# An adaLN and MoE block in fp32: the condition mixing's products in three fp32r passes, one table buffer, new instruction orders

## The reference

```python
# stage 0: a condition vector of each sequence makes a 128x128 matrix of rank 30
t   = x @ U(cond_512) + ub(cond_512)            # U from W_dec, b_dec;  [tokens, 30]
x0  = t @ V                                      # what the experts and the gate see
g   = top2_softmax(x0 @ Wg.T + bg)               # 8 experts, 2 used, computed densely
x1  = x + sum_e g_e * (gelu(x0 @ W1[e].T + b1[e]) @ W2[e].T + b2[e])
# stage 1: six conditions mixed by softmax(aw), three by tables, three by small MLPs
h   = layernorm(x1)
t_, s_, h_ = h * tm_g[ic], h * ms_g[im], layernorm(h * pw_g[ip] + pw_b[ip]) * cp_g[ic]   # rows of tables
z   = x1 @ Wx + t_ @ Wt + s_ @ Ws + h_ @ Wh + one-hot terms + terms of the sequence
y   = layernorm(silu(z) @ int_W2 + int_b2) * int_g + int_be
u   = silu(y @ w1 * s1) * (y @ w2 * s2)          # ternary weights
out = x1 + (gelu(gelu(u @ h1 * sh1) @ h2 * sh2) @ w3) * s3
```

## Time and profile before

| | |
|---|---|
| median of 3 runs | 433.07 us (431.69 to 435.24) |
| the profiled execution, its time | 432.53 us |
| the same, first to last instruction (span) | 430.6 us |
| busy PE, VectorE, ScalarE, GpSimd | 412.8, 313.0, 291.9, 115.1 us |
| granted TensorE clock, mean | 0.988 of full speed |

### The profile page before, as it was taken

The page is one execution under the profiler, slowest core; times in us unless marked ns, Lnnn a source line. Parts: engine busy times, 40 slices in busy tenths (PEclk is TensorE's granted clock), DMA queues, the critical chain, the costliest instruction groups (busy, mean ns, idle before and its releaser), DMA issues.

```text
span 430.6 us, 5742 instructions
## 1 busy us (share of the span) xinstructions
PE 412.8 (96%) x1804; PEld 270.1 (63%) x1804; DVE 313.0 (73%) x656; ACT 291.9 (68%) x518; POOL 115.1 (27%) x122
## 2 busy tenths in 40 slices
PE   6988999999999999999999999999999999898995
PEld 3755555545566765776567655776577657677774
DVE  4897899988995587658866757677963798656643
ACT  3687867877756864677646784786578475757653
POOL 0048102443525610244153000457035031110000
PEclk9996899999999999999999999999999999999999
DMA  6986547553443341334530260336402210000000
GB/s 232 356 355 210 140 102 193 138 171 105 128 124 107 107 129 50 105 73 107 141 99 32 57 164 0 89 69 175 153 0 65 73 56 0 2 0 24 2 24 27
DMA packets 30216, 45.07 MB, mean 105 GB/s; under 512 B 3717, under 2 KB 22634, under 8 KB 29674
## 3 DMA queue, kind: packets, MB, share of 16 engines
q1 hardware_dynamic: 25792, 32.88, 26.6%
q0 software_dynamic: 3584, 10.49, 7.5%
q10 hardware_dynamic: 810, 1.33, 0.9%
HBM read 40.68 MB, written 4.03 MB: 104 GB/s over the span
## 4 chain that ended last, share of the span: by engine, by line
PE 77%; DVE 9%; DMA 6%; issue 3%; ACT 3%; SPq 1%; POOL 1%; DVEq 0%; ACTq 0%; POOLq 0%
PE bank L752 21%; PE bank L650 20%; PE bank L788 7%; PE bank L698 7%; PE bank L642 5%; PE bank L737 5%; DMA gwbs<-gate_w 3%; PE bank L666 2%; PE bank L705 2%; DMA t_split<-tsS 2%; PE bank L830 2%; PE bank L777 1%; DMA Wd<-W_dec_in 1%; SPq L417 1%; PE bank L711 1%
## 5 line engine op out<-in xcount | busy, mean ns | idle before, releaser
L650 PE MATMUL bank<-mG,W 128*128 128x512 f32 x256 | 121.4, 600 | 0.2 <-DVE mG L1186 0.2
L897 ACT ACTIVATE mG<-bank,keepP 128x512 f32<-128x512 f32 x128 | 85.2, 687 | 29.3 <-PE bank L642 19.1
L1460 POOL TENSOR_TENSOR rstd<-ve,mhalf 128x4 f32<-128x4 f32 x24 | 32.7, 1364 | 206.3 <-DVE ve L1201 206.2
L1186 DVE TENSOR_TENSOR mG<-mG,gwbs 128x1024 f32<-128x1024 f32 x64 | 77.3, 1218 | 3.0 <-DMA gwbs<-gate_w 2.5
L650 PEld LDWEIGHTS bank<-mG,W 128*128 128x128 f32 x256 | 48.0, 192 | 40.0 <-issue 35.6
L642 PE MATMUL bank<-ts,A 96*128 96x512 f32 x128 | 64.5, 546 | 1.4 <-DVE A L1308 0.7
L962 ACT ACTIVATE G<-bank,keepP 128x512 f32<-128x512 f32 x48 | 32.1, 691 | 27.9 <-PE bank L752 27.8
L1441 POOL DMA_INDIRECT gp<-pgb_in,ixall x32 | 35.7, 1114 | 26.6 <-issue 9.2
L752 PE MATMUL bank<-hB_h,h2w_h 128*128 128x512 f32 x96 | 39.8, 414 | 0.0
L752 PE MATMUL bank<-hA_h,h1w_h 128*128 128x512 f32 x96 | 38.7, 403 | 0.0
L1444 POOL DMA_INDIRECT gcm<-ctm,ixcm x32 | 35.4, 1108 | 9.7 <-issue 9.4
(11 more groups left out here) (241 smaller groups left out, 775.8 us busy)
## 6 DMA issues: line engine op xcount, KB each, us to landing
gwbs<-gate_w SPq DMA_DIRECT2D x32, 512.0 KB
keep<-xT_in SPq DMA_DIRECT2D x8, 256.0 KB, 6.1
outT<-keep SPq DMA_DIRECT2D x8, 256.0 KB, 2.0
t_split<-tsS SPq DMA_DIRECT2D x7, 192.0 KB
ts<-t_split SPq DMA_DIRECT2D x7, 192.0 KB
W1T<-W1T_in SPq DMA_DIRECT2D x1, 1024.0 KB, 10.5
W<-W2T_in SPq DMA_DIRECT2D x1, 1024.0 KB, 13.3
hs<-h1T_in SPq DMA_DIRECT2D x1, 1024.0 KB, 11.6
```

The lines of the kernel that those rows point to most:

```text
L650: mm = pe.matmul(OACC[:, :], W2[:, e * HC + c, :], mG[n % NMG][:, c, :], start=False, stop=(e == E - 1 and c == HC - 1))
L897: act.activation(mG[e % NMG][:, c % HC, :], HM[n % 2][:, :], ACT.Gelu, bias=b1c[:, c:c + 1]).then_inc(m_gelu, 1)
L1186: dve.tensor_tensor(mine, mine, gate.unsqueeze(1).broadcast_to([P, HC, TT, P]), ALU.mult).then_inc(m_q, 1)
L1460: step(pool.tensor_tensor(rstd[:, n, :], ve[:, n, :], mhalf[:, :], ALU.pow))
```

## The change

- In Z, t, s and h are split like the feed-forward's data: ScalarE's copy out of XE writes the fp32r part (`turned_hi`), a new VectorE step (`tl`, `sl`, `hl`) the rest (`turned_lo`), also from XE. Z has three fp32r products for each (weight high by data high, high by low, low by high) in place of one fp32 product; the product with x1 stays in fp32 (`wx`). XE is free for the next turn when `tl`, `sl` or `hl` is done. `zl` splits the weights once, behind a copy on ScalarE.
- One buffer for the gathered tables instead of two; the place goes to `turned_lo`. The gathers of block b wait until t, s and h of block b-1 have been made.
- W_dec is the first load on SyncE's queue; the two small loads that stood before it are first on ScalarE's.
- All orders are written anew. Weight splits `wl` go in another sequence. A step `filler` is defined, but stands in no order.

The diff, its orders cut to those that are spoken of:

```diff
         w3 = [sb(f"w3_{p}", [P, FC, P], F32R) for p in "hl"]
-        wmix = sb("wmix", [P, 4, P])
+        wx = sb("wx", [P, P])
+        wc = [sb(f"wc_{p}", [P, 3, P], F32R) for p in "hl"]
...
         wsc = sb("wsc", [P, 6, P], stack=early)
+        wcf = sb("wcf", [P, 3, P], stack=early)
...
         mG = [mGs[:, i * HC:(i + 1) * HC, :] for i in range(NMG)]
-        gcm, gp = [None, None], [None, None]
-        gcm[0] = sb("gcm0", [P, TT, 3 * P])
-        gp[0] = sb("gp0", [P, TT, 2 * P])
+        gcm = sb("gcm", [P, TT, 3 * P])
+        gp = sb("gp", [P, TT, 2 * P])
...
         xh, tt, ss, hh = [norms[:, i, :, :] for i in range(4)]
-        ct, cs_, ch = [sb(f"c{k}", [P, T]) for k in "tsh"]
+        turned_hi = [sb(f"c{k}_h", [P, T], F32R) for k in "tsh"]
...
         nmr = sb("nmr", [P, 3, TT])
-        gp[1] = sb("gp1", [P, TT, 2 * P])
-        gcm[1] = sb("gcm1", [P, TT, 3 * P])
+        turned_lo = [sb(f"c{k}_l", [P, T], F32R) for k in "tsh"]
+        sb("spare", [P, 992])
...
         tr_mm = sems("tt_mm", "ss_mm", "hh_mm")
-        tr_out = sems("t_out", "s_out", "h_out")
+        tr_out, tr_lo = sems("turned_hi", "turned_lo")
+        wc_hi, wc_lo = sems("wc_hi", "wc_lo")
...
                 "y_mm", "yT_mm", "f_full", "f_hi", "f_lo")
-        gat = sems("gat0", "gat1")
+        gat = sems("gat")[0]
...
-            eng.wait_ge(w_lo, max((4, 2, 1, 3)[n] for n in ns))
+            eng.wait_ge(w_lo, max((1, 3, 4, 2)[n] for n in ns))
...
         ORDER = {
...
-                (3, "H0 -O5 ~F1 H1 H2 -O6 H3 H4 ~F2 =Ts -O7 H5 H6 =Th ~F3 -XT B =Z ~F4 ~F5 H7 ~F6 H8 =Y ~F7 H9 O0 O1 ~F8 H10 H11 "
-                    "~F9 ~F10 =YT ~F11 O2 H12 O3 -Tt H13 H14 ~F12 H15 =F0 -Ts O4"),
...
+                (0, "A0 tm0 tm1 gm0 A1 sq0 tm2 A2 tm3 A3 gx0 sq1 H0 tm4 gm1 H1 H2 H3 H4 tm5 H5 gm2 H6 sq2 H7 B gm3 O0 H8 H9 O1 H10 "
+                    "O2 H11 H12 sq3 H13 O3 H14 H15 tm6"),
+                (1, "H0 gx1 -O4 H1 -O5 -O6 H2 H3 -O7 H4 H5 tm7 H6 -XT B gm4 H7 O0 H8 H9 H10 O1 H11 O2 H12 gm5 O3 H13 -Tt H14 H15"),
+                (2, "H0 -O4 H1 -O5 H2 =Ts gm6 gm7 H3 H4 -O6 H5 -O7 =Th gx2 H6 =Z low -XT B H7 H8 =Y br"),
+                (2, "H9 O0 O1 -Tt =YT O2 H10 H11 O3 H12 H13 =F0 H14 H15 O4 -Ts"),
+                (3, "H0 H1 ~F1 H2 -O5 H3 -O6 ~F2 =Th H4 -O7 H5 ~F3 =Z H6 -XT B O0 ~F4 H7 ~F5 ~F6 ~F7 H8 =Y O1 H9 -Tt ~F8 ~F9 H10 "
...
+                (7, "H0 H1 =Th -O7 H2 ~F3 =Z H3 -XT ~F4 H4 ~F5 ~F6 B ~F7 O0 H5 =Y -Tt H6 ~F8 ~F9 ~F10 H7 =YT ~F11 H8 H9 O1 -Ts O2 "
+                    "H10 ~F12 =F0 H11 H12 -Th O3 H13 =F1 -Z =F2 H14 O4 -Y H15 =F3 O5 O6 O7 -YT XT =F4 -Fr0 =F5 -Fr1 =F6 Tt =F7 -Fr2 "
+                    "Ts =F8 Th =F9 Z -Fr3 =F10 Y =F11 -Fr4 -Fr5 YT -Fr6 -Fr7 Fp0 =F12 Fp1 -Fr8 Fp2 -Fr9 Fp3 -Fr10 -Fr11 Fp4 Fp5 Fp6 "
+                    "Fp7 -Fr12 Fp8 Fp9 Fp10 Fp11 Fp12"),
...
-                (0, "am tb0 sv2 al0 tb1 top0 sv0 gww0 tb2 sv1 gxl0 al1 gl tb3 sv3 sv6 tb4 al2 al3 bl sv4 q0 tcl3 q1 tb5 q2 top1 "
-                    "tcl4 q3 q4 gww1 sv5 q5 wl2 gxl1 tcl5 sml0 sml1 q6 wl1 q7 wl3 wl0 sml2"),
-                (1, "q0 -x q1 -st0 q2 q3 tb6 tb7 q4 q5 tcl6 -hg q6 tcl7 -t q7 top2 -s -oh -hc gww2 x gxl2 st0"),
-                (2, "q0 q1 =a lm q2 =st2 la -oh q3 q4 -t q5 =flo -hg =u0 q6 =fl0 -s =u1 q7 -hc =u2 x"),
...
+                (0, "gl al0 tb0 am tb1 sv2 top0 sv0 al1 gww0 tb2 sv1 gxl0 al2 al3 tb3 sv3 tb4 bl sv6 wl0 sv4 tcl3 q0 q1 q2 top1 q3 "
+                    "tcl4 q4 sv5 gww1 sml0 tb5 q5 q6 gxl1 wl3 q7 wl1 wl2 tcl5 x sml1"),
+                (1, "q0 q1 -st0 sml2 zl tb6 q2 q3 q4 -t -hg q5 -tl tb7 tcl6 q6 -s -hc tcl7 q7 top2 -sl gww2 -oh -hl gxl2"),
+                (2, "q0 q1 lm -x la =a -st0 =st2 -t q2 q3 q4 -tl -s =flo -hg =u0 q5 q6 -sl =u1 -hc q7 =u2 -hl -oh"),
+                (3, "q0 ~fl0 -x ~u3 ~fl1 ~fl2 ~fl3 -st0 =a q1 -t -s ~fl4 ~fl6 =st2 -oh -hg q2 -tl ~fl8 q3 ~fl10 q4 =flo q5 ~fo -hc "
...
+                (7, "q0 q1 =a -st0 -t ~fl4 ~fl6 =st2 -hg -oh q2 q3 -s -tl ~fl8 ~fl10 =flo q4 -sl -hc ~fo =u0 -hl =u1 q5 =fl0 -a q6 "
+                    "=u2 -st2 =fl1 q7 =u3 =fl2 x =fl3 st0 -flo oh -ur0 t s hg -ur1 tl =fl4 =fl6 hc sl -flr0 -flr1 hl -ur2 =fl8 a "
+                    "-ur3 -flr2 -flr3 st2 =fl10 flo -flr4 up0 =fo -flr6 up1 up2 flp0 flp1 up3 flp2 flp3 -flr8 -flr10 flp4 flp6 flp8 "
+                    "flp10 -for flp11 fop"),
...
-                (2, "tab0 tab1 tab2 rt0 tab3"),
...
+                (1, "tab0 tab1 tab2 tab3 rt0 -rt2 rt1"),
+                (2, "tab0 tab1 tab2 rt0 tab3 -rt2 rt1"),
...
-                (0, "sgw0 sgp0 sts1 gb0 lr gb1 +lt sts2 sts3 gb2 gb3 sgw1 sgp1"),
...
+                (0, "sts1 sgw0 sgp0 gb0 lr gb1 +lt sts2 gb2 sts3 gb3 sgw1"),
...
-            load(gap[:, KA + 2 * KR + 1:KA + 2 * KR + 3], A["keepP"][0:2, 0:2].unsqueeze(0).broadcast_to([MU, 2, 2]), ld_wd)
-            load(muT[:, :], A["cond_512T"].unsqueeze(1).broadcast_to([MU, 2, B]), ld_wd)
...
                     pe.matmul(XL[:, 0:P], syT[:, n * B:(n + 1) * B], wsc[:, 2 + n, :], start=(n == 0), stop=(n == 2))
-                for n, w_ in enumerate((3, 1, 2)):
-                    mm = pe.matmul(XE[0:NI, 3 * P:4 * P], tbT[:, n, :], wmix[:, w_, :], start=(n == 0), stop=(n == 2))
+                for n, w_ in enumerate((2, 0, 1)):
+                    mm = pe.matmul(XE[0:NI, 3 * P:4 * P], tbT[:, n, :], wcf[:, w_, :], start=(n == 0), stop=(n == 2))
...
                 if b:
-                    pe.wait_ge(tr_out[2], b)
+                    pe.wait_ge(tr_lo, 3 * b)
...
                 pe.wait_ge(s_ready, b + 1)
-                pe.wait_ge(tr_out[0], b + 1)
+                pe.wait_ge(tr_lo, 3 * b + 1)
...
                 pe.wait_ge(h_ready, b + 1)
-                pe.wait_ge(tr_out[1], b + 1)
+                pe.wait_ge(tr_lo, 3 * b + 2)
...
                 pe.wait_ge(x1_ready, b + 1)
-                for m, src in enumerate((keep[b % 3], ct, cs_, ch)):
-                    if m:
-                        pe.wait_ge(tr_out[m - 1], b + 1)
-                    mm = pe.matmul(XL[:, :], wmix[:, m, :], src[:, :], start=False, stop=(m == 3))
+                pe.matmul(XL[:, :], wx[:, :], keep[b % 3][:, :], start=False, stop=False)
+                if b == 0:
+                    pe.wait_ge(wc_lo, 1)
+                for m in range(3):
+                    pe.wait_ge(tr_lo, 3 * b + m + 1)
+                    for n, (w_, c) in enumerate(((0, turned_hi), (0, turned_lo), (1, turned_hi))):
+                        mm = pe.matmul(XL[:, :], wc[w_][:, m, :], c[m][:, :], start=False, stop=(m == 2 and n == 2))
...
-            steps = {"low": lambda i: low(), "br": lambda i: None, "B": B_, "H": H_, "O": O_, "XT": XT, "Tt": Tt, "Ts": Ts, "Th": Th, "Z": Z, "Y": Y, "YT": YT,
+            def filler():
+
+                pe.matmul(OACC[:, :], Uall[:, 0:P], Uall[:, 0:T], start=True, stop=True)
+
+            steps = {"low": lambda i: low(), "fi": lambda i, n: filler(), "br": lambda i: None, "B": B_, "H": H_, "O": O_, "XT": XT, "Tt": Tt, "Ts": Ts, "Th": Th, "Z": Z, "Y": Y, "YT": YT,
...
             def turned_out(b, n):
-                dst = (ct, cs_, ch)[n]
+                dst = turned_hi[n]
...
                     act.wait_ge(small_src, NSMALL)
-                act.activation(dst[:, :], XE[:, :], ACT.Copy).then_inc(tr_out[n], 1)
+                act.activation(dst[:, :], XE[:, :], ACT.Copy).then_inc(tr_out, 1)
...
                 act.activation(wint[:, :], iW2, ACT.Copy, scale=0.5)
-                for n, dst in enumerate((wmix[:, 3, :], wmix[:, 1, :], wsc[:, 2, :], wsc[:, 3, :], wsc[:, 4, :], wmix[:, 2, :])):
+                for n, dst in enumerate((wcf[:, 2, :], wcf[:, 0, :], wsc[:, 2, :], wsc[:, 3, :], wsc[:, 4, :], wcf[:, 1, :])):
...
                 ins.then_inc(wsc_ready, 1)
+                act.wait_ge(wsc_ready, 1)
+                act.activation(flat(wc[0]), flat(wcf), ACT.Copy).then_inc(wc_hi, 1)
...
+            load(gap[:, KA + 2 * KR + 1:KA + 2 * KR + 3], A["keepP"][0:2, 0:2].unsqueeze(0).broadcast_to([MU, 2, 2]), ld_wd)
+            load(muT[:, :], A["cond_512T"].unsqueeze(1).broadcast_to([MU, 2, B]), ld_wd)
...
                 src, dst = staged[n], split[n]
-                dve.wait_ge(w_hi, (3, 1, 2, 4)[n])
+                dve.wait_ge(w_hi, (1, 3, 4, 2)[n])
...
                 dve.wait_ge(normed[0], b + 1)
-                dve.wait_ge(gat[b % 2], (b // 2 + 1) * 16 * 2 * TT)
+                dve.wait_ge(gat, (b + 1) * 16 * 2 * TT)
...
                     dve.wait_ge(tr_mm[2], b)
-                pw = gp[b % 2]
+                pw = gp
...
             def t_(b):
-                dve.wait_ge(gat[b % 2], (b // 2 + 1) * 16 * 2 * TT)
+                dve.wait_ge(gat, (b + 1) * 16 * 2 * TT)
...
                     dve.wait_ge(tr_mm[0], b)
-                dve.tensor_tensor(tt[:, :, :], xh[:, :, :], gcm[b % 2][:, :, P:2 * P], ALU.mult).then_inc(t_ready, 1)
+                dve.tensor_tensor(tt[:, :, :], xh[:, :, :], gcm[:, :, P:2 * P], ALU.mult).then_inc(t_ready, 1)
...
             def s_(b):
```

(50 more changed lines are left out.)

8 lines of the change are left out of this document (1 added, 7 removed), and 96 rows, old and new, of the table ORDER.

## The result

| | before | changed |
|---|---|---|
| median of 6 runs each | 433.01 us (431.69 to 435.24) | 449.64 us (448.19 to 450.85) |
| ratio, 95% interval | | 1.039 (1.036 to 1.042) |
| profiled execution: time, span | 432.53, 430.6 us | 449.64, 447.8 us |
| mean granted clock of TensorE | 0.988 | 0.969 |
| idle PE in the span | 17.8 us | 26.9 us |

A forecast was written before the change was run, and what follows sets the result against it. PE's amount of work bounds the middle, DVE the stretch 19.5 to 89 us. -4.0 + 1.3 - 0.6 + 0 + 0 = -3.3 from 433.07 gives 429.8 us; range 425.0 to 435.5.

The forecast's parts named there:

- Part 1: Z: three fp32 products become nine fp32r ones, 0.51 us less per block, 4.1 us in eight blocks, taken as 4.0.
- Part 2: DVE's added subtractions: covered in the middle, not in the DVE-bound start; between 0 and +2.6 us, taken as +1.3.
- stand ahead of block 1's `x`: DVE at the start: the low-part steps, 2.6 us, come before `x`, itself ahead of B, XT and the next O.
- if that cover were gone: Middle: no O, F or H steps covering XE's longer hold between turns; 0.7 us per turn, 24 turns, 17 us.
- Rival 3: Start: the new orders also close PE's holes there, and W_dec's full 1.6 us is possible; 426.0 us, chance 0.25.
- Part 3: Start: W_dec is issued 1.6 us earlier, b_dec perhaps later; between +0.5 and -1.6 us, taken as -0.6.
- Part 4: Gathers wait for the previous block's tables: hidden, except perhaps at block 2's `t`, 0 to 4 us; taken as 0.
- single table buffer: Slower: DVE waits 4 us at t(2) or its like, passed on whole, plus 2.6 at the start; 435.9 us, chance 0.13.
- Part 5: Tail: `t` of block 7 comes earlier, but Ts(7) may wait; between -2.0 and +1.8 us, taken as 0.
- a stretch to Z(0) longer by more than 3 us: Start, up to block 0's Z: one of the signs that would show the forecast wrong, size 3 us.
- Rival 1: Start: Z's gain goes into DVE, costing 2.6 us, with b_dec 0.5 and the tail 0.5; 432.7 us, chance 0.22.

The follow-up runs named there:

- e_filler: The changed kernel with five unused 128x512 products added to PE's order of block 0: 449.34 us, 1.036.
- the last version: The kernel before with Z's three passes, s turned in another bank, block 0's h in a third, and three turns of DVE's order moved: 433.42 us, 0.997.

## Why the prediction was wrong

**Part 1, Z: right.** The block shown gains 0.60 us, but one block isn't all: from the start of Z to the product behind it the eight blocks take 30.8 us before and 27.7 after, 3.1 less. Another 1.2 comes back right behind Z, where in three blocks of the kernel before (1, 6 and 7) an fp32r product takes 0.63 us to the next start; behind Z in the changed one it is 0.23. Together that is 4.2 us, forecast 4.0. The starts are 0.23 us apart, but the first fp32r product, behind the fp32 one, takes 0.64, so from first to last it is 2.24 us and not 2.0. DVE is busy 329.5 us (forecast 328 to 332), and there is no fp32 record but those of `keep`. In 145 to 300 us PE is never idle.

**Part 2, DVE's added work: the size failed, by seven to ten times, because it was priced by its busy time.** The step that failed is the one in which `zl`, `tl`, `sl` and `hl`, 2.6 us, "stand ahead of block 1's `x`" and the middle between 0 and 2.6, +1.3, is taken. It counts DVE's microseconds; what counted is who waits behind each. A turn bank is free when `tl` is done, and `tl` stands in a queue: 3.90 us of PE for 0.68 us of work. With the orders of before, two table buffers and one bank, the passes cost 9.4 us net (443.31 against 433.88), some 14 gross with the 4.2 us that Z saves; in the changed kernel's orders about 4.6 net (1.0391 against 1.0284) and some 9 gross. The case "if that cover were gone" was in the text at 0.7 us per turn, but its price is that of a whole queue. Its place depends on the order: in the changed kernel no turn in the middle has a hole before it, as was forecast, and the start has them; with the old orders the middle has them too (4.5 us idle in 130 to 350 us). More banks and moved steps take nearly all of it back with DVE's busy time unchanged, which shows the cause. By the ladder: 1.023, 1.013, 1.007, 0.997.

**The clock behind the holes was not in the sum at all.** Rival 3 had it only as something to win. In the changed kernel, (1 - mean clock) times span grows from 5.2 to 13.9 us, by 8.7; idle PE grows by 9.1; the saving is 4.2; together 13.6 of the 17.2 us of span. The other 3.6 stay open; matmul ends are modelled. The spells lie at 17.2 to 24, 41 to 55 and 95.7 to 102.5 us; before there was one, 35.4 to 45.7. But this part isn't independent: in e_filler (1 - mean clock) times span is 11.0 us, 2.9 less, and a spell begins 6 us later, without a gain. That fits a slow PE costing time only where the others wait for PE, but doesn't show it, since the fillers take some 4 us of PE themselves.

**Part 3, W_dec first: right in its sign of risk, wrong in its bound.** The worst case was b_dec 1.6 us later, for +0.5. It comes 3.7 us later (16.12 against 12.43 in the earlier trace rows). The wait is for two loads of b_dec. Its 15 KB are issued 1.3 us later on ACT's queue (2.73 instead of 1.42) and land 8.5 us after the issue instead of 2.2, at about 11.2 us. What comes last is the other, of 0.1 KB: issued at 5.47 instead of 3.80, it lands 10.6 us later instead of 8.6. SyncE's large loads stand 1.6 us earlier on their queue. The Trainium skill, "DMA: Bandwidth & Descriptors", section "Queues, rings and completion order", says that each DMA engine goes round its queues packet by packet; the late landings of the small loads, 8.5 and 10.6 us, agree with that. Alone it costs 5.2 us; in the changed kernel about 1 or nothing (449.64 against 448.63), because there the first `O` waits for more than U.

**Part 4, one buffer: 3.7 us where I took 0.** I looked for the wait at t(2) and its root; in the changed kernel t(2) (150.79) doesn't wait. It is one block earlier: the gathers of block 1 wait for `hc(0)`, which is late in the slow start, and the root of block 1 is queued behind them on GpSimd. The rival "single table buffer" had the mechanism and the sign, with another place. The work it needs does fit in the middle.

**Part 5, orders: the largest single term, taken as 0.** Without the passes the new orders cost 1.9%, 8 to 10 us, on top of the buffer. With the passes they are level with the plain old ones (1.039 against 1.043), so the terms don't add: the new orders give the turns cover, and cost it elsewhere. Where elsewhere is read from the trace and not isolated. Most of the loss is there by the first `O` (43.7 and 49.49 us without the passes), and the changed kernel shows a chain that leads to it. `tcl2` on GpSimd comes 7.4 us later than before (29.05):

```profile
33.39 1.31 POOL L1464 DMA_INDIRECT gp<-pgb_in,ixall  x1 [1.67 <-PE bank L820]
35.00 0.95 POOL L1467 DMA_INDIRECT gcm<-ctm,ixcm  x1 [0.30 <-issue]
36.48 1.27 POOL L1477 TENSOR_TENSOR tsS<-tT,tsS 32x512 fp32r<-32x512 f32 x1 [0.54 <-ACT tsS L866]
```

It stands behind the first two gathers, but it waits 0.54 us more behind them, for ACT's `tch2`, which the new order has put behind `ah3` and `ws` and which begins at 35.78 (28.29 before). Moving `tcl2` alone ahead of the gathers would thus gain nothing. The store behind `tcl2` goes out at 38.07 instead of 34.78. ACT then waits for that store at `tch4`, which stands ahead of the gelus that H7 needs:

```profile
45.61 0.63 ACT L866 ACTIVATE tsS<-tT 32x512 fp32r<-32x512 f32 x1 [3.26 <-remote]
...
46.86 0.79 PE L644 MATMUL bank<-ts,A 96*128 96x512 f32 x1 [1.64 <-issue]
...
49.18 1.20 PE L652 MATMUL bank<-mG,W 128*128 128x512 f32 x1
```

The second row is H7. H7, B and `gm3` stand ahead of the first `O`, the third row, whose data the first `q` has ready at about 44.9. The version with new orders and no passes has the same waits (3.76 us at 45.93 on ACT, 1.90 us at 47.18 on PE); with the old orders `tch4` comes behind the first `O` and doesn't wait. An experiment that moves only `tch2`, `tch4` or the first `O` was not made.

**The ladder of the changed kernel**, each step against the kernel before: one buffer 1.009; new orders as well 1.028; passes as well 1.039; late small loads as well 1.039. The intervals of the new orders without and with the passes overlap (1.020 to 1.036 and 1.033 to 1.045, both with the small loads on SyncE), so the passes' 1% there is likely rather than sure. In microseconds (the differences of the ratios, times 433) the buffer is some 4 where 0 was taken, the orders 8 where 0 was taken, the passes with all that hangs on them +4.6 where +1.3 - 4.0 = -2.7 was taken, and W_dec 0 to 1 where -0.6 was taken. As steps of a ladder they add up to the measured 16.6 by construction, and another sequence of steps would share it out otherwise.

**Signs named beforehand:** first `tm` 16.4 to 18.4 (22.08, wrong), Z(0)'s end 93 to 97 (110.2, wrong by 13 us), "a stretch to Z(0) longer by more than 3 us" (14.3: the sign of error that was named), holes ahead of Ts and Th in the middle (none). That the middle gets some 3 us shorter can't be told, as the new orders move steps between blocks: from Z(1) to the last `O` it is 232.2 us before and 232.6 after, from B(3) to the last `O` 232.6 and 228.4. Rival 1 had the right place and about a sixth of the price (3.6 of some 21 us); rival 3, that the new orders close the holes of the start, had the wrong sign. Its text gives PE "some 16 us of work in all before the first O", which is too low: PE is busy 32.9 of the first 41.4 us, 18.4 of them from 19.5 us on.

**Open:** which step of the new orders costs the 8 to 10 us; the 3.6 us left in the account; and why of the 4.2 us saved in Z only about 1 arrives in the last version. In its profile XT(0) is 2.2 us later than in the kernel before (69.3 against 67.1), Z(1) 2.9 us and the end 1.0 us, so behind Z(1) it does gain 1.9 us.

## What to carry to other kernels

Price a step by what its wait holds, not by its busy time: a 0.7 us subtraction that keeps a PSUM bank busy can cost as much as everything queued ahead of it on its engine; here a second bank and earlier turns took that back. A change that gains in the steady middle must be read at the start and the end as well, where no other block's work covers a wait; check each small load's queue against the large ones issued just before it. One buffer instead of two moves its cost to whatever is queued behind the transfer's issue, here a root on GpSimd.

## What the runs showed of the hardware that was not expected

- The clock falls behind several small holes, not only behind a long one. With two banks, PE waited 0.88, 0.34 and 0.90 us between 89 and 93 us, and the granted clock was 0.62 on the mean of the next 9 us; with three banks there were two holes, 0.28 and 0.49 us at 89.9 and 91.3 us, and it stayed at 1.00. These rows are with two banks:

```profile
90.11 0.66 PE L676 MATMUL bank<-keepP,tsh 128*128 128x128 f32 x4 [0.88 <-issue]
...
91.34 0.66 PE L676 MATMUL bank<-keepP,tsh 128*128 128x128 f32 x4 [0.34 <-issue]
...
93.12 0.33 PE L600 MATMUL bank<-keepP,gw 128*128 128x128 f32 x1 [0.90 <-DVE gw L1198]
```

- At half clock PE shows as busy. In the changed kernel, these 2 us in a row have 11 records at clock 0.50 and no idle time, so the busy share doesn't show the loss; the clock column does.

```profile
96.00:98.00 2.00, 2.00 (x11) 2.00 (x11) 1.94 (x4) 1.18 (x2) 1.02 (x1) 0.50 0.01 3
```

- An fp32r product directly behind an fp32 one takes 0.63 to 0.64 us to the next start, and 0.23 behind another fp32r one. So each passage from fp32 to fp32r costs some 0.4 us, wherever it lies.
- A load of 15 KB landed 2.2 us after its issue, and 8.5 us after it when it was issued 1.3 us later and the large loads of another queue 1.6 us earlier. One of 0.1 KB landed 8.6 and 10.6 us after its issue in the same two traces.
